# A transformer block on one core: value projection moved, fills removed, strip copies and strip transposes reordered

## The chip, the cores and the metric

The kernel runs on one core of one Trainium2 chip. The metric is the device time of one execution in microseconds (us), as the median of several runs. All times below are in us from the first instruction of the profiled execution, unless they are marked ns.

## What is computed

Eight sequences of 256 token ids go through an embedding and one transformer block of width 256 with 16 heads of 16, in float32:

```python
h = onehot(x) @ embeddings                               # (8, 256, 256)
# attention, H = 16 heads, hd = 16, rotary embedding of q and k
q, k, v = split(layernorm(h) @ w_qkv)
attn = softmax((rope(q) @ rope(k).T) * hd ** -0.5)
h = h + (attn @ v).reshape(B, N, D) @ w_proj
# mixture of experts, E = 8, the best-scored expert alone
y = layernorm(h)
chosen = argmax(y @ gate_w.T)
h = h + y + expert_w[chosen] @ y
```

## The kernel before

**Batches as a pipeline.** Each of the eight sequences is a batch `b` of NT = 2 tiles of 128 tokens. Products that need float32 accuracy are made from a high and a low part of each operand: `product` (L484) issues three matmuls for each of the two 128-row halves of the contraction. The work on a batch is spread over several steps: in step `b` TensorE makes the transposed scores of batch `b`, whose exponentials ScalarE takes (`exp`, L889), the plain scores of batch `b + 1`, whose maxima VectorE takes (`maximum`, L1027), the projections of batch `b + 2`, the end of the attention and the gate of batch `b - 1`, and the experts of batch `b - 2`. A pass numbered -1 goes before step 0, and steps 8 and 9 empty the pipeline.

**Slots set the order.** Every engine has its own program, and each walks through 16 slots per step. Tables (`FRONT`, `EARLY`, `TWO`, `FOUR` for the projections of a batch, `POST` and `LAST` for what follows the attention) name the slot in which an item is issued, on whichever engines have a part in it. Within a slot the order is that of the lines of each engine's `step`. Engines run strictly in that order and wait for one another by semaphores, so an instruction that waits holds up all that stands behind it on its engine.

**TensorE's step (L749).** Even slots hold a `visit` (L645): the scores of two heads, 8 matmuls. A visit waits for VectorE's maxima and ScalarE's exponentials of the visit before (L581, L624). In step 0 each visit is followed by fills (L491, L755), matmuls into `m_bank` whose result is not read: 3, then 4, then 1 each. Slots 5, 9 and 13, and slot 1 of the next step, hold `outputs` (L666), the product of exponentials and values for four heads; ScalarE copies its strips from `o_bank` to `o_t` (`outputs`, L897) in slots 6, 10 and 14 and in slot 1. The same bank's other half takes the transposes of the maxima (`max_transpose`, L613) in slot 3 and in slot 10 or 11; those wait for the copies of groups 1 and 3. In slot 11 of steps 0 and 1 the projection of q and k of a later batch follows, which waits for VectorE's `x_low` (L998).

**After the attention of a batch `k`,** in step `k + 1`: `o_transpose` (L681) turns the strips of tile 0 in slot 2 (`o0`) and of tile 1 in slot 4 (`o1`), both into `m_bank` except for tile 1 of batch 0 (`strips_bank`, L266), so tile 1 waits for VectorE's `o_norm` (L1042) of tile 0, which is in slot 3; `o_norm` of tile 1 is in slot 5. Then `on_transpose` (slot 6), `o_high` and `o_low` (L903, L1051), `out_project` (slot 8), `residual` and the second normalisation `g_norm` (slots 9 to 11), `y_transpose` (slot 12). A unit of experts (`experts`, L734) stands in each even slot of steps 2 to 6, in other slots from step 7 on; within a slot it comes after `o_transpose` of tile 1 and after `project_v`.

**The value projection** `project_v(b)` (L509) has 12 matmuls of 128x256. For batch 2 it stands in slot 7 of step 0 (`TWO`), goes to `f_bank` (`v_bank`, L217), and ScalarE's `values` (L850) copies it to `vals`. In step 0, slot 9, `x_transpose(3)` (L496) goes to `f_bank` too; it waits for VectorE's `xn` (L992), which in turn stands behind `max_split` (L1034) of slot 7. SyncE moves the maxima's rows and the restacked q and k by DMA (`maximum`, L292, `restack`, L314).

Of the kernel before, what the change touches and what calls it, by code (L numbers as in the profile page):

```python
# [36 lines left out]
def tower(nc, x, emb, w_qkv, w_proj, gate_w, expert_w, rope, ramp, out):  # L37
# [12 lines left out]
    with ExitStack() as ctx:  # L50
# [77 lines left out]
        def pair_of_banks(name):  # L128
# [6 lines left out]
        f_bank = bank("f_bank")  # L135
        o_bank = bank("o_bank")
        m_bank = bank("m_bank")
        e_bank = bank("e_bank")
# [37 lines left out]

        FRONT = dict(stats=-8, norm=-6, x=-5, x_low=-4, qk0=-3, qk1=-1, rotate0=-2, rotate1=0, t0=1, low0=2, t1=3, low1=4, v=5)
        EARLY = dict(stats=-12, norm=-9, x=-7, x_low=-6, qk0=-5, qk1=-4, rotate0=-3, rotate1=-2, t0=0, low0=1, t1=2, low1=3, v=5)
        TWO = dict(rotate0=0, rotate1=1, t0=2, low0=3, t1=4, low1=5, v=7)
        FOUR = dict(FRONT, stats=-10, norm=-8, x=-7, x_low=-6, qk0=-5, rotate0=-3, qk1=-2, v=-3)  # L180
        POST = dict(o0=2, o1=4, norm0=3, norm1=5, on=6, o_low=7, proj=8, residual=9, stats=10, g_norm=11,
                    y=12, y_low=13, gate=14, gate_t=15, choose=15)
        LAST = dict(o0=2, o1=2, norm0=3, norm1=3, on=4, o_low=5, proj=6, residual=7, stats=7, g_norm=8,
                    y=9, y_low=10, gate=11, gate_t=12, choose=12)
# [15 lines left out]
        def here(b, k):  # L200

            return 0 <= b + k < NB
# [12 lines left out]
            return m_bank if k in (1, 2) else f_bank  # L215

        def v_bank(k):  # L217
            return o_bank if k < 2 else e_bank if k == 4 else f_bank

        def x_parts(k):  # L220
            return (y_h[0], y_l[0]) if k == 1 else (x_h, x_l)
# [258 lines left out]
        def _(pe):  # L480
# [10 lines left out]
            def fill(o, n):  # L491

                for i in range(n):
                    mm(o[:, :], wqkv_h[:, 0, 0:P], wqkv_h[:, 0, 0:512], start=True, stop=True)
# [14 lines left out]
            def project_v(b, tiles=range(NT)):  # L509
                if tiles[0] > 0:  # L510
                    pass
                elif b == 4:
                    wait(pe, xl_ok, b + 1)
                    wait(pe, on_ok, NT)
                elif b >= 2:
                    wait(pe, qkl_ok, (b - 1) * NT + NT)
                elif b == 1:
                    wait(pe, v_ok, b)
                else:
                    pe.wait_ge(z_in, z_copied(1, 3))  # L520
                x_h, x_l = x_parts(b)
                for t in tiles:
                    m = product(v_bank(b)[:, t * D:(t + 1) * D], lambda c: x_h[:, c, t, :], lambda c: x_l[:, c, t, :],
                                lambda c: wqkv_h[:, c, 2 * D:3 * D], lambda c: wqkv_l[:, c, 2 * D:3 * D])
                if tiles[-1] == NT - 1:
                    m.then_inc(v_ps, 1)
# [86 lines left out]
            def max_transpose(b, u):  # L613

                wait(pe, o_ok, (b - 1) * GROUPS + (4 if u else 2))
                if b == 0:
                    pe.wait_ge(v_ok, 2)
                wait(pe, ml_ok, b * 2 + u + 1)
                for t in range(NT):
                    m = tr(o_bank[0:16, N + t * P:N + (t + 1) * P].bitcast(F32R),  # L620
                           max_parts[:, u, t, :, :, :].rearrange("p i a j -> p (i a j)"), ident_r[:, :])
                m.then_inc(mt_ps, 1)
# [126 lines left out]
            def step(b, p):  # L749
                for s in range(SLOTS):  # L750
                    g_at = SLOTS * b + s
                    if s % 2 == 0:
                        visit(b, s // 2)
                        if b == 0:
                            fill(m_bank, 3 if s == 0 else 4 if s == 2 else 1)  # L755
                    if here(b, 0) and s == 3:
                        max_transpose(b, 1)
                    if here(b, 1) and s == maxima_slot(b + 1):
# [74 lines left out]
            fill(m_bank, 1)  # L833
            visit(-1, 7)
            project_qk(2, 1, [1])
            fill(m_bank, 2)
            steps(step)


        @block.scalar  # L840
        def _(act):
# [80 lines left out]
            def step(b, p):  # L922
                for s in range(SLOTS):
                    g_at = SLOTS * b + s
                    if here(b, 0) and s % 2 == 0:
                        exp(b, s // 2)
                    if here(b, 0) and s == 3:
                        max_row(b, 1)
                    if here(b, -1) and s == 1:
                        outputs(b - 1, 3)  # L930
                    for k in batches(front, "x", g_at):
                        x_high(k)
                    if here(b, 0) and s in (6, 10, 14):
                        outputs(b, (s - 6) // 4)
                    for k in batches(post, "on", g_at):
                        o_high(k)
                    for t in range(NT):
                        for k in batches(front, f"t{t}", g_at):
                            qk_high(k, t)
                        for k in batches(front, f"low{t}", g_at):  # L940
                            qk_high_again(k, t)
                    for k in batches(front, "v", g_at):
                        values(k)
                    if here(b, 1) and s == maxima_slot(b + 1):
                        max_row(b + 1, 0)
                    for k in batches(post, "y", g_at):
                        y_high(k, k % 2)
                    for k in batches(post, "gate", g_at):
                        gate_row(k)
                    if b < 2 and s % 4 == 1:  # L950
                        expert_weights(4 * b + s // 4)
# [309 lines left out]
```

## Time and profile before

| | us |
|---|---|
| median of 3 runs | 303.5 |
| lowest and highest | 303.13, 305.42 |
| profiled execution, device time | 303.43 |
| its span, first to last instruction | 301.6 |

The page of the profile gives TensorE 278.1 us of busy time (92% of the span), VectorE 242.2 (80%), ScalarE 132.5 (44%) and GpSimd 88.7 (29%). The granted TensorE clock is 1.000 over the span. Of the chain that ended last 63% lies on TensorE, 25% on VectorE and 5% on ScalarE. TensorE's matmuls are pipelined and overlap, so a busy share of 92% says that something is always in flight, not that it works at its peak. A visit can be found in a timeline as a pair of rows L640 and L599; a row's idle time in brackets is that of its engine just before it, with the instruction that ended it. From visit 0 to visit 0, steps 3 and 4 take 33.0 us each, step 0 takes 22.3.

### The profile page before, as it was taken

How to read it: one execution, taken by the hardware profiler on the slowest of the kernel's cores; microseconds unless marked ns; L12 is line 12 of the kernel's file. 1: busy time of each engine (PE TensorE's matmuls, PEld its weight loads, DVE VectorE, ACT ScalarE, POOL GpSimd, SP SyncE). 2: the span in 40 equal slices, each digit the busy share in tenths (PEclk: the TensorE clock that was granted, in tenths of full speed). 3: DMA queues.
4: the chain of work that ended last, by engine and by line, in shares of the span. 5: the costliest groups of instructions: out<-in, count | busy, mean ns of one | idle time of the engine just before them, and what ended most of it. 6: DMA issues, size and time to landing. Idle time of an engine off the chain costs nothing.

```text
span 301.6 us, 5654 instructions
## 1 busy us (share of the span) xinstructions
PE 278.1 (92%) x2068; PEld 199.2 (66%) x2068; DVE 242.2 (80%) x602; ACT 132.5 (44%) x271; POOL 88.7 (29%) x105
## 2 busy tenths in 40 slices
PE   2798999898898999999999999999999999999895
PEld 2577666555576676777667776777667666667584
DVE  8698899698879898879978798869888965557765
ACT  3165438667465442553336443643433455330100
POOL 5735628184334042502240132202200300210400
PEclk9999999999999999999999999999999999999999
DMA  4440625905800840176003900193010010010011
GB/s 120 147 190 8 168 51 95 132 8 98 120 1 13 147 65 2 43 120 95 4 2 90 149 12 2 37 158 54 5 36 2 2 37 3 3 35 0 0 37 35
DMA packets 10803, 17.55 MB, mean 58 GB/s; under 512 B 2024, under 2 KB 4883, under 8 KB 10648
## 3 DMA queue, kind: packets, MB, share of 16 engines
q1 hardware_dynamic: 9988, 16.62, 27.5%
q0 software_dynamic: 768, 0.55, 0.8%
q8 instruction: 17, 0.28, 0.5%
q14 instruction: 10, 0.08, 0.1%
q10 hardware_dynamic: 20, 0.02, 0.0%
HBM read 5.30 MB, written 2.10 MB: 25 GB/s over the span
## 4 chain that ended last, share of the span: by engine, by line
PE 63%; DVE 25%; ACT 5%; issue 4%; POOL 2%; DVEq 0%; POOLq 0%
PE e_bank L488 19%; PE f_bank L488 10%; PE o_bank L676 9%; DVE neg_max L1030 6%; PE t_pair L640 5%; DVE acc L1128 4%; PE s_pair L488 4%; PE m_bank L488 3%; PE s_pair L599 2%; PE m_bank L690 2%; PE m_bank L722 2%; ACT probs L894 1%; POOL h L376 1%; PE m_bank L698 1%; ACT parts L843 1%
## 5 line engine op out<-in xcount | busy, mean ns | idle before, releaser
L894 ACT ACTIVATE probs<-t_pair 128x512 f32<-128x512 f32 x128 | 69.5, 595 | 85.9 <-PE t_pair L640 85.5
L1030 DVE TENSOR_REDUCE neg_max<-s_pair 128x2 f32<-128x512 f32 x120 | 76.9, 683 | 9.7 <-PE s_pair L599 9.5
L640 PE MATMUL t_pair<-stacks 50*128 50x256 f32 x256 | 46.8, 308 | 1.6 <-DVE neg_max L1030 0.8
L640 PEld LDWEIGHTS t_pair<-stacks 50*128 50x128 f32 x256 | 32.8, 185 | 23.4 <-issue 21.5
L599 PE MATMUL s_pair<-stacks 48*128 48x256 f32 x240 | 44.8, 309 | 0.2 <-ACT stacks L843 0.2
L488 PE MATMUL e_bank<-ew_h,y_h 128*128 128x512 f32 x92 | 40.2, 437 | 1.9 <-DVE acc L1128 1.5
L1128 DVE SCALAR_TENSOR_TENSOR acc<-e_bank,mask,acc 128x256 f32<-128x256 f32 x66 | 28.9, 479 | 11.6 <-PE e_bank L488 11.5
L488 PE MATMUL e_bank<-ew_l,y_h 128*128 128x512 f32 x92 | 36.3, 395 | 0.0
L488 PE MATMUL e_bank<-ew_h,y_l 128*128 128x512 f32 x92 | 36.2, 393 | 0.0
L406 POOL TENSOR_TENSOR qk<-rope_a,rope_b 128x512 f32<-128x512 f32 x16 | 20.8, 1300 | 48.3 <-DVE rope_b L1017 48.3
L676 PE MATMUL o_bank<-probs,vals 128*32 128x256 f32 x512 | 34.3, 385 | 0.0
L599 PEld LDWEIGHTS s_pair<-stacks 48*128 48x128 f32 x240 | 31.3, 185 | 0.9 <-issue 0.4
L488 PEld LDWEIGHTS e_bank<-ew_h,y_h 128*128 128x128 f32 x92 | 17.3, 188 | 9.0 <-DVE acc L1128 3.9
L412 POOL TENSOR_SCALAR g_ve<-g_mv 128x2 f32<-128x2 f32 x8 | 2.0, 246 | 68.9 <-DVE g_mv L986 68.9
L676 PEld LDWEIGHTS o_bank<-probs,vals 128*32 128x32 f32 x512 | 13.4, 109 | 12.4 <-issue 5.4
L488 PEld LDWEIGHTS e_bank<-ew_l,y_h 128*128 128x128 f32 x92 | 17.3, 188 | 4.0
L376 POOL DMA_INDIRECT h<-in_emb,ids x16 | 17.8, 1110 | 5.6 <-issue 3.1
L843 ACT ACTIVATE o_t<-o_bank 128x256 f32<-128x256 f32 x32 | 12.5, 390 | 14.7 <-PE o_bank L676 14.7
L488 PEld LDWEIGHTS e_bank<-ew_h,y_l 128*128 128x128 f32 x92 | 17.4, 189 | 2.1
L488 PE MATMUL f_bank<-wqkv_h,x_h 128*128 128x512 f32 (+1 forms) x42 | 15.1, 360 | 0.6 <-DVE x_l L1001 0.4
L423 POOL TENSOR_TENSOR res<-acc 128x256 f32<-128x256 f32 x14 | 10.3, 735 | 16.4 <-DVE acc L1128 16.4
L488 PE MATMUL f_bank<-wqkv_h,x_l 128*128 128x512 f32 (+1 forms) x42 | 14.3, 341 | 0.0
(182 smaller groups left out, 554.5 us busy)
## 6 DMA issues: line engine op xcount, KB each, us to landing
stacks<-parts SPq DMA_DIRECT2D x36, 256.0 KB, 6.8
ew_raw<-in_expert_w SPq DMA_DIRECT2D x1, 2048.0 KB, 8.4
out<-res SPq DMA_DIRECT2D x7, 256.0 KB
stacks<-parts SPq DMA_DIRECT2D x12, 128.0 KB, 3.3
probs<-in_w_qkv SPq DMA_DIRECT2D x2, 384.0 KB, 3.1
stacks<-max_rows SPq DMA_DIRECT2D x30, 8.0 KB
h<-in_emb,ids POOLq DMA_INDIRECT x16, 7.3
probs<-in_w_proj SPq DMA_DIRECT2D x1, 256.0 KB
```

The costliest lines, as they stand in the source:

```text
L376: g.indirect_dma_start(h0[:, j, :], None, emb, bass.IndirectOffsetOnAxis(ap=ids[:, j:j + 1], axis=0), bounds_check=V - 1, oob_is_err=False ...
L406: g.tensor_tensor(turned, rope_a[:, t, :, :].rearrange("p (g j) d -> p g j d", j=j), rope_b[:, t, :, :].rearrange("p (g j) d -> p g j d", ...
L423: g.tensor_tensor(res[:, t, :], acc[:, 0, t, :], acc[:, 1, t, :], ALU.add).then_inc(res_ok, 1)
L488: m = mm(o, a(c), w(c), start=(c == 0 and n == 0), stop=(c == C - 1 and n == 2))
L599: m = mm(scores_pair(b, v)[:, half, t * N:(t + 1) * N], stacks[b % STACKS][r:r + KS, pair, 0, t * P:(t + 1) * P], stacks[b % STACKS][r:r + ...
L640: m = mm(t_pair[:, half, c * N:(c + 1) * N], stacks[b % STACKS][r:r + KM, pair, 1, c * P:(c + 1) * P], stacks[b % STACKS][r:r + KM, pair, ...
L676: m = mm(o_bank[STRIP * j:STRIP * (j + 1), 0:N], vals_flat[b % VALS][:, at:at + STRIP], probs[:, (4 * g + j) % RING, c, :], start=(c == 0) ...
L690: m = tr(strips_bank(b, t)[:, g * P:(g + 1) * P], o_t[:, g, t * P:(t + 1) * P], ident[:, :])
L843: return nc.scalar.activation(o, i, ACT.Copy)
L894: nc.scalar.activation(probs[:, (2 * v + half) % RING, :, :].rearrange("p c n -> p (c n)"), t_pair[:, half, :], ACT.Exp, scale=SCALE).then ...
L1030: v.tensor_reduce(neg_max[:, k // 4, :, 4 * half + k % 4], scores_pair(b, k)[:, half, :].rearrange("p (t n) -> p t n", t=NT), AX.X, ALU.ma ...
L1128: v.scalar_tensor_tensor(out=acc[:, j, t, :], in0=y, scalar=mask[:, p, t, e:e + 1], in1=base[:, t, :] if u == 0 else acc[:, j, t, :], op0= ...
```

## The change

Four edits.

1. `project_v(2)` leaves slot 7 of step 0. Its tile 0 is issued just before step 0, in place of two fills, and its tile 1 after visit 0, in place of three fills. It goes to `o_bank` instead of `f_bank`, waits for the values of batch 1 to be copied, and ScalarE copies its result after the first exponentials of step 0. The max transpose of slot 3 in step 0, which writes to `o_bank`, waits for that copy.
2. Of step 0's other fills (4 after visit 1, one after each of the six visits after it) three remain after visit 1 and none elsewhere.
3. ScalarE's copies of the output strips in slots 6, 10 and 14 of all steps stand before the exponentials of their slot instead of after them.
4. The strips of tile 1 are turned in slot 5 instead of slot 4, for all batches but the last.

```diff
--- before.py
+++ after.py
@@ -176,9 +176,9 @@
 
         FRONT = dict(stats=-8, norm=-6, x=-5, x_low=-4, qk0=-3, qk1=-1, rotate0=-2, rotate1=0, t0=1, low0=2, t1=3, low1=4, v=5)
         EARLY = dict(stats=-12, norm=-9, x=-7, x_low=-6, qk0=-5, qk1=-4, rotate0=-3, rotate1=-2, t0=0, low0=1, t1=2, low1=3, v=5)
-        TWO = dict(rotate0=0, rotate1=1, t0=2, low0=3, t1=4, low1=5, v=7)
+        TWO = dict(rotate0=0, rotate1=1, t0=2, low0=3, t1=4, low1=5)
         FOUR = dict(FRONT, stats=-10, norm=-8, x=-7, x_low=-6, qk0=-5, rotate0=-3, qk1=-2, v=-3)
-        POST = dict(o0=2, o1=4, norm0=3, norm1=5, on=6, o_low=7, proj=8, residual=9, stats=10, g_norm=11,
+        POST = dict(o0=2, o1=5, norm0=3, norm1=5, on=6, o_low=7, proj=8, residual=9, stats=10, g_norm=11,
                     y=12, y_low=13, gate=14, gate_t=15, choose=15)
         LAST = dict(o0=2, o1=2, norm0=3, norm1=3, on=4, o_low=5, proj=6, residual=7, stats=7, g_norm=8,
                     y=9, y_low=10, gate=11, gate_t=12, choose=12)
@@ -215,7 +215,7 @@
             return m_bank if k in (1, 2) else f_bank
 
         def v_bank(k):
-            return o_bank if k < 2 else e_bank if k == 4 else f_bank
+            return o_bank if k < 3 else e_bank if k == 4 else f_bank
 
         def x_parts(k):
             return (y_h[0], y_l[0]) if k == 1 else (x_h, x_l)
@@ -512,9 +512,9 @@
                 elif b == 4:
                     wait(pe, xl_ok, b + 1)
                     wait(pe, on_ok, NT)
-                elif b >= 2:
+                elif b >= 3:
                     wait(pe, qkl_ok, (b - 1) * NT + NT)
-                elif b == 1:
+                elif b >= 1:
                     wait(pe, v_ok, b)
                 else:
                     pe.wait_ge(z_in, z_copied(1, 3))
@@ -614,7 +614,7 @@
 
                 wait(pe, o_ok, (b - 1) * GROUPS + (4 if u else 2))
                 if b == 0:
-                    pe.wait_ge(v_ok, 2)
+                    pe.wait_ge(v_ok, 3)
                 wait(pe, ml_ok, b * 2 + u + 1)
                 for t in range(NT):
                     m = tr(o_bank[0:16, N + t * P:N + (t + 1) * P].bitcast(F32R),
@@ -751,8 +751,10 @@
                     g_at = SLOTS * b + s
                     if s % 2 == 0:
                         visit(b, s // 2)
-                        if b == 0:
-                            fill(m_bank, 3 if s == 0 else 4 if s == 2 else 1)
+                        if b == 0 and s == 0:
+                            project_v(2, [1])
+                        if b == 0 and s == 2:
+                            fill(m_bank, 3)
                     if here(b, 0) and s == 3:
                         max_transpose(b, 1)
                     if here(b, 1) and s == maxima_slot(b + 1):
@@ -833,7 +835,7 @@
             fill(m_bank, 1)
             visit(-1, 7)
             project_qk(2, 1, [1])
-            fill(m_bank, 2)
+            project_v(2, [0])
             steps(step)
 
 
@@ -922,16 +924,18 @@
             def step(b, p):
                 for s in range(SLOTS):
                     g_at = SLOTS * b + s
+                    if here(b, 0) and s in (6, 10, 14):
+                        outputs(b, (s - 6) // 4)
                     if here(b, 0) and s % 2 == 0:
                         exp(b, s // 2)
+                    if b == 0 and s == 0:
+                        values(2)
                     if here(b, 0) and s == 3:
                         max_row(b, 1)
                     if here(b, -1) and s == 1:
                         outputs(b - 1, 3)
                     for k in batches(front, "x", g_at):
                         x_high(k)
-                    if here(b, 0) and s in (6, 10, 14):
-                        outputs(b, (s - 6) // 4)
                     for k in batches(post, "on", g_at):
                         o_high(k)
                     for t in range(NT):
```

## Rows read from the trace of the kernel before

**Rows 1.** Step 0: busy time by engine, granted clock, DMA share, GB/s

```profile
40.40:63.10 22.70, 20.22 (x168) 13.46 (x167) 19.35 (x38) 15.02 (x31) 11.27 (x11) 1.00 0.49 76
```

**Rows 2.** Timeline of TensorE in step 0: start, length, instruction, idle before

```profile
41.64 0.96 PE L494 MATMUL m_bank<-wqkv_h 128*128 128x512 f32 x3
...
42.77 0.35 PE L640 MATMUL t_pair<-stacks 50*128 50x256 f32 x1 [0.17 <-DVE neg_max L1030]
...
43.80 1.20 PE L494 MATMUL m_bank<-wqkv_h 128*128 128x512 f32 x4
...
49.76 0.28 PE L488 MATMUL f_bank<-wqkv_h,x_h 128*128 128x256 f32 x1
...
51.29 0.38 PE L640 MATMUL t_pair<-stacks 50*128 50x256 f32 x1
...
52.89 0.63 PE L506 MATMUL f_bank<-ident,xn 128*128 128x128 f32 x4 [0.43 <-DVE xn L995]
...
54.45 0.38 PE L640 MATMUL t_pair<-stacks 50*128 50x256 f32 x1
...
55.12 0.50 PE L494 MATMUL m_bank<-wqkv_h 128*128 128x512 f32 x1
...
56.40 0.29 PE L620 MATMUL o_bank<-ident_r,max_parts 128*16 128x128 f32 x2 [0.78 <-ACT o_t L843]
...
63.06 0.35 PE L640 MATMUL t_pair<-stacks 50*128 50x256 f32 x1 [0.33 <-DVE neg_max L1030]
```

**Rows 3.** Timeline of VectorE in step 0

```profile
46.10 0.69 DVE L1022 TENSOR_TENSOR parts<-f_bank,parts 128x512 fp32r<-128x512 f32 x1 [0.49 <-ACT parts L843]
...
50.67 1.21 DVE L1037 CAST max_parts<-neg_max 128x16 fp32r<-128x16 f32 x1
...
58.64 1.29 DVE L1030 TENSOR_REDUCE neg_max<-s_pair 128x2 f32<-128x512 f32 x2 [2.33 <-PE s_pair L599]
```

**Rows 4.** Timeline of ScalarE in step 0

```profile
49.36 1.06 ACT L894 ACTIVATE probs<-t_pair 128x512 f32<-128x512 f32 x2
...
51.40 0.60 ACT L843 ACTIVATE vals<-f_bank 128x512 f32<-128x512 f32 x1 [0.70 <-PE f_bank L488]
...
55.95 0.39 ACT L843 ACTIVATE o_t<-o_bank 128x256 f32<-128x256 f32 x1
```

**Rows 5.** Timeline of TensorE, step 1, slots 10 to 12

```profile
80.67 0.29 PE L620 MATMUL o_bank<-ident_r,max_parts 128*16 128x128 f32 x2 [1.21 <-ACT o_t L843]
...
83.01 0.66 PE L714 MATMUL m_bank<-ident,yn 128*128 128x128 f32 x4
```

**Rows 6.** Timeline of VectorE, the same stretch

```profile
79.06 0.66 DVE L1001 TENSOR_TENSOR x_l<-f_bank,x_h 128x512 fp32r<-128x512 f32 x1
...
81.29 0.74 DVE L1070 TENSOR_SCALAR yn<-h,g_mv,g_rs 128x256 f32<-128x256 f32 x2 [0.38 <-POOL g_rs L414]
```

**Rows 7.** L690's idle time by releaser (us, times); TensorE in step 3

```profile
  DVE o_n L1047: 4.9, 10
...
129.16 0.66 PE L690 MATMUL m_bank<-ident,o_t 128*128 128x128 f32 x4 [0.40 <-DVE o_n L1047]
...
132.56 1.07 PE L676 MATMUL o_bank<-probs,vals 128*32 128x256 f32 x16
```

**Rows 8.** Timeline of VectorE in step 3, slot 5

```profile
131.24 0.88 DVE L1128 SCALAR_TENSOR_TENSOR acc<-e_bank,mask,acc 128x256 f32<-128x256 f32 x2 [0.34 <-PE e_bank L488]
```

**Rows 9.** Timeline of ScalarE in step 3, slot 6

```profile
134.10 1.09 ACT L894 ACTIVATE probs<-t_pair 128x512 f32<-128x512 f32 x2 [0.83 <-PE t_pair L640]
```

**Rows 10.** Timeline of TensorE in step 7, slot 8

```profile
255.63 0.38 PE L488 MATMUL m_bank<-wp_h,o_h 128*128 128x256 f32 x1 [0.25 <-DVE o_l L1053]
```

**Rows 11.** Fills of the start: ns min/median/max, first and last start

```profile
L494 PE MATMUL s_pair<-wqkv_h x13: 387/592/767, 5.3 to 9.6; 128*128 128x512 f32 x13
```

**Rows 12.** Busy times and granted clock, 10.0 to 13.4

```profile
10.00:13.40 3.40, 1.80 (x9) 1.28 (x10) 2.44 (x8) 0.70 (x2) 2.88 (x4) 1.00 0.60 165
```

**Rows 13.** Timeline of SyncE's queue at the end of step 0

```profile
57.12 1.37 SPq L297 DMA_DIRECT2D stacks<-max_rows  x2
```

## The prediction

> **What bounds the kernel now.** I read the profile in this order: the busy shares by stretch, the chain that ended last, then the timelines of TensorE, VectorE and ScalarE beside each other for one step of each kind (step 0, step 1, one of the alike steps 2 to 6, step 7), each time asking who ended TensorE's idle time. In a stretch of 22.7 us that holds step 0, TensorE is busy 20.22 us and VectorE 19.35 us [rows 1], so neither alone sets the pace; the chain changes from one to the other. Part of TensorE's busy time there is fills, matmuls whose result nobody reads: 3 after visit 0, 4 after visit 1, one after each later visit, 13 in step 0 and 2 more just before it [rows 2]. From step 2 on TensorE has next to no idle time but 0.4 us per step before the transposes of the second tile's strips [rows 7]. So TensorE sets the end from step 2 on, and in steps 0 and 1 a chain through all three engines does.
>
> **Step 0, slots 0 to 4.** The projection v(2) (12 matmuls of 128x256) leaves slot 7, where it holds TensorE from 49.76 to the next visit at 51.29, 1.53 us, together with its bank change from f_bank to o_bank. Its first half takes the place of two fills before visit 0, its second half that of the three fills after it. Three fills last 0.96 us there, and half of v is 0.77 us, so TensorE is at visit 1 no later; and visit 1 ended an idle time of 0.17 us that VectorE's maxima released [rows 2], so this costs nothing; without that cover it would cost at most the 0.3 us by which 0.77 exceeds two fills (0.48). ScalarE gets the copy into vals, 0.60 us [rows 4], between the first exponentials: the second pair comes some 0.3 us later. Visit 2 waits for that pair, but only 2 us after it; nothing is lost. The maxima's transpose of slot 3 now waits for that copy too; behind it TensorE's whole queue would stand, but the copy ends near 43.2 and the transpose is due at 45. The fourth fill after visit 1 goes: 1.20 minus 0.96 is 0.24 us. That one counts, since ScalarE's high part, and behind it VectorE (idle 0.49 us at 46.10 [rows 3]), waits for the transposes issued after the fills. I take 0.2 us.
>
> **Step 0, slots 6 to 10.** Without v and the fill, visit 4 no longer waits for TensorE but for the exponentials of visit 3 (49.36 plus 1.06 us [rows 4]): its second half can go near 50.5, where before the whole visit began at 51.29. That gain of nearly 1 us is not kept: VectorE's split of the maxima (50.67, 1.21 us for a 128x16 cast [rows 3]) and its xn stand in front of the x transposes of slot 9 at 52.89, which TensorE waited for by 0.43 us anyway [rows 2]. What is kept there is the 0.2 us from above (bounds: nothing, if the long cast ends when it ended before; the whole 1.2 us, if it shrinks to the ordinary length).
>
> Now the copies. In slot 10 the max transpose waits for the copy of output group 1. Before, that copy stood behind both exponentials of visit 5: it began at 55.95, and TensorE, done with the visit at 55.12 and with one fill after it, sat idle 0.78 us until 56.40 [rows 2, 4]. The strips are finished when visit 5 begins (54.45), so a copy in front takes 54.5 to 54.9, less the 0.2, and ends before the visit does. The transpose follows the visit: 56.40 minus 55.12 is 1.28 us, minus 0.03 of latency, plus the 0.2: 1.45 us. VectorE had been idle 2.33 us behind this (58.64 [rows 3]), so it takes over the whole 1.45. From there to visit 0 of step 1 (63.06) VectorE is busy without a break; the fills of slots 12 and 14 are worth nothing. **Step 0: 1.45 us.**
>
> **Step 1.** In slot 6 the copy in front lets o_high start 0.26 us earlier (a copy's 0.39 us less the overlap), of which the split of the maxima leaves about 0.2. In slot 10 TensorE waited 1.21 us for the copy of group 1, until 80.67 [rows 5]. Without that, the next limits are VectorE's x_low, done at 79.72, which releases qk(4,0), and yn, done at 82.03, which releases the y transposes (83.01 before) [rows 5, 6]. The latter leaves 0.9 us. **Step 1: 0.9 + 0.2 = 1.1 us.**
>
> **Steps 2 to 6, the second tile's strips.** The two tiles' strips share m_bank, so the second turn must wait until VectorE has normalised the first, and in slot 4 TensorE stood for that: 0.40 us at 129.16; the view lists ten such waits, five on the matmul row and five on the weight row [rows 7], one pair for each of the five steps. With the turn in slot 5 the unit of experts of slot 4 comes first; it waits for nothing here, since the select before it is over. Then come the four transposes, v(k) and the output group. Nothing is added; 0.40 us of standing goes. Who waits for the strips now? VectorE's second normalisation, which stands behind a select begun at 131.24 [rows 8] that itself now starts 0.35 us sooner; experts (1.5 us) and transposes (0.6) end some 2.1 us after the visit, near 130.9, and that select ends near 131.7. VectorE then waits for visit 3 in any case, so TensorE keeps its gain. In step 1 no work lies between slots 4 and 5 and the order stays; in step 7 likewise, for its experts stand in odd slots. **5 x 0.40 = 2.0 us** (bounds: 0, if the wait only changes its name; 2.5, if each step saves the wait and 0.1 us of restart after it).
>
> **The copies in steps 2 to 7.** A copy ahead of the exponentials could delay them. It does not: the output group begins at 132.56 and lasts 1.07 us, the exponentials begin at 134.10 after 0.83 us of idle time [rows 7, 9]; the copy needs 0.26 us before the next can follow and starts near 133.7. It has no gain either, but in step 7: there the out projection stood 0.25 us for o_low [rows 10], which hangs on ScalarE's o_high behind that copy. **0.25 us.**
>
> **Sum:** 1.45 + 1.1 + 2.0 + 0.25 = 4.8 us. The profiled execution took 303.43 us (span 301.6); minus 4.8 is 298.6. The median of the three runs is 303.5, so the same number holds for it.
>
> **The rivals.** *The strips' gain moves on* (0.12): VectorE's second normalisation is late and the next transposes wait as long. Then 303.4 - 2.8 = 300.6. For it: VectorE is also nearly full; against it: it waits for visit 3 after that normalisation.
> *Step 0 gives little* (0.10): the transfer of the maxima's rows, issued from 57.12 in 1.37 us behind the restack's transfers [rows 13], is needed (by visit 0 of step 1, 63.06) 1.45 us earlier but issued only 1 us earlier, since the row copy still stands behind both exponentials; or the cast takes back what came. Step 0 and 1 then give 1.2 instead of 2.5: 299.9.
> *The clock falls once* (0.08). TensorE's work from 49.3 to 52.7 shrinks to one visit of 0.7 us, and an idle time of about 1.7 us stands before the x transposes. The thinnest stretch of the trace, 1.80 us busy of 3.40, was granted 1.00 (2.4 GHz) [rows 12], so the rows speak against it but do not reach that far. The price: of the 13 fills of the start the last began 4.3 us after the first, with a median of 592 ns against 387 at the fastest [rows 11]; 12 spacings of 0.24 us would be 2.9. So 1.4 us and a little for the shorter work between: 1.6 us, and 300.2.
> The Trainium skill (TensorE: Matmul & The Clock Gate, Part 1) says that half rate is the default and that recent activity releases it, which speaks against taking fills out; by that rule this case comes about, and with it those 300.2 us.
> *Slower than before* (0.04): the clock falls there and stays low. From 52.7 to about 60 TensorE sets the pace with some 7 us of work. At 1.2 GHz it costs its own length again: 7 us, so 305.6. It decides from 4.8 us of work at the low level on.
> *More than summed* (0.08): the long cast disappears or the fills had cost others: 1.2 us more, 297.4.
>
> **How the numbers follow.** The forecast has the remaining 0.58, with its own range of 298.0 to 299.2. With the rivals, 297.3 to 300.7 leaves out the lasting clock fall and tails, under 2 in 10. A measurement of this kernel tells about 1% from no change, 3 us here: faster means below 300.5. The forecast, the larger gain, the little step 0 and half of the cases at 300.2 and 300.6 lie there, and some unknown is taken off: 0.81. Within 1%: 0.14. Slower: 0.05.
>
> **What the profile after would show.** Visit 0 of step 1 near 61.6. No wait for o_t before the max transposes of slot 10. No o_n idle before m_bank's strips in steps 2 to 6, and periods of 32.6 us in place of 33.0 (129.16 to its like). Granted clock 1.00 from 49 to 56. The prediction falls if that clock is lower, if visit 0 of step 1 waits for the transfer, or if a new wait of 0.3 us or more stands in slots 5 or 6 of steps 2 to 6.

## The result, and the profile after

| us | before | after |
|---|---|---|
| median of 10 runs each, on one chip | 303.56 | 300.38 |
| lowest and highest of after | | 299.73, 302.31 |
| profiled execution of after | 303.43 | 300.52 |
| its span | 301.6 | 298.7 |
| granted clock over its span | 1.000 | 0.989 |

The ratio is 0.9884, with a 95% interval from 0.9861 to 0.9907: the change saves 3.2 us of the 4.8 that were summed. The time lies inside the range (297.3 to 300.7), but not where the likeliest case put it (298.0 to 299.2). It lies where the rival "the clock falls once" did, at 300.2, and that rival had a chance of 0.08.

The page of the profile of after has a row of the granted clock (the span in 40 slices of 7.5 us, tenths of full speed), and it shows one dip. Before, it has none.

```profile
PEclk9999998699999999999999999999999999999999
```

The windows around it, of the kernel after (window, length, busy us of TensorE, its weight loads, VectorE, ScalarE and GpSimd with instruction counts, granted clock, DMA share, GB/s), to be set beside [rows 1], which reads 1.00 for all of step 0:

```profile
44.40:48.40 4.00, 3.69 (x40) 2.30 (x38) 3.74 (x9) 3.48 (x8) 3.53 (x4) 1.00 0.07 18
48.40:50.40 2.00, 1.09 (x12) 0.65 (x8) 1.97 (x5) 1.96 (x5) 1.92 (x3) 0.99 0.65 171
50.40:52.40 2.00, 0.85 (x6) 0.53 (x4) 1.97 (x5) 1.20 (x2) 1.32 (x2) 0.50 1.08 153
52.40:54.40 2.00, 1.85 (x12) 1.11 (x16) 1.30 (x4) 0.73 (x2) 0.00 (x0) 0.50 1.06 152
54.40:56.40 2.00, 2.00 (x20) 1.12 (x12) 0.69 (x2) 0.91 (x3) 1.27 (x1) 0.50 1.04 154
56.40:58.40 2.00, 2.00 (x12) 1.37 (x8) 1.19 (x2) 1.19 (x3) 0.00 (x0) 0.80 1.05 153
58.40:60.40 2.00, 2.00 (x14) 1.56 (x14) 1.31 (x3) 1.28 (x3) 0.00 (x0) 1.00 0.28 37
```

The clock is at its lower level, 1.2 GHz (0.50), from about 50.4 to 57, and back at 2.4 GHz behind that. TensorE's timeline of the same stretch shows what stood before the fall and what it cost. These rows of after answer to [rows 2]:

```profile
49.97 0.35 PE L640 MATMUL t_pair<-stacks 50*128 50x256 f32 x1 [0.82 <-ACT probs L896]
50.17 0.28 PE L640 MATMUL t_pair<-stacks 50*128 50x256 f32 x1
50.46 0.55 PE L640 MATMUL t_pair<-stacks 50*128 50x256 f32 x1
50.81 0.42 PE L640 MATMUL t_pair<-stacks 50*128 50x256 f32 x1
...
52.55 1.08 PE L506 MATMUL f_bank<-ident,xn 128*128 128x128 f32 x4 [1.30 <-DVE xn L999]
53.57 1.94 PE L676 MATMUL o_bank<-probs,vals 128*32 128x256 f32 x16
...
56.59 0.38 PE L620 MATMUL o_bank<-ident_r,max_parts 128*16 128x128 f32 x2
...
63.52 0.35 PE L640 MATMUL t_pair<-stacks 50*128 50x256 f32 x1 [0.98 <-DVE neg_max L1034]
```

Two idle times, 0.82 and 1.30 us, frame visit 4 (49.97). The clock fell between the two halves of this visit: the first two matmuls have their ordinary 0.35 and 0.28 us, the next two take 0.55 and 0.42. So in this execution the second gap came too late to be a cause of the fall. The x transposes behind it take 1.08 us where they took 0.63, the output group 1.94 where it takes 1.07 at the full clock. The wait for `o_t` in front of L620 (0.78 before) is gone, as forecast, yet L620 starts at 56.59 instead of 56.40: what the copies gave back, the clock took. Visit 0 of step 1 starts at 63.52, before it was 63.06.

From there on the sum comes out. I took the starts of the 32 output groups (L676, four to a batch) in both traces and their differences, after minus before. For the groups of step 0 they go from -0.38 to +0.44 and for those of step 1 from +0.45 to -0.69. At the first group of steps 2 to 6, which stands just behind the strips, they are -1.12, -1.46, -1.90, -2.27 and -2.61, and in step 7 they go from -2.63 to -2.89. So step 1 gives 1.13 us (1.1 summed), the five steps with strips 1.92 (2.0 summed), step 7 0.26 (0.25 summed). TensorE and VectorE after, in step 1, slot 10, which answer to [rows 5] and [rows 6]:

```profile
79.62 0.29 PE L620 MATMUL o_bank<-ident_r,max_parts 128*16 128x128 f32 x2
80.01 0.51 PE L488 MATMUL f_bank<-wqkv_h,x_h 128*128 128x512 f32 x1
...
82.33 0.66 PE L714 MATMUL m_bank<-ident,yn 128*128 128x128 f32 x4
```

```profile
79.29 0.66 DVE L1005 TENSOR_TENSOR x_l<-f_bank,x_h 128x512 fp32r<-128x512 f32 x1
...
81.54 0.74 DVE L1074 TENSOR_SCALAR yn<-h,g_mv,g_rs 128x256 f32<-128x256 f32 x2 [0.39 <-POOL g_rs L414]
```

The 1.21 us for `o_t` are gone. `x_l` ends at 79.95 and releases the next projection at 80.01, `yn` ends at 82.28 and releases the y transposes at 82.33, 0.68 us earlier than before, although the step was entered 0.45 us late. These are the two limits that the prediction named.

The strips of the second tile, in the groups of instructions of L690 (busy, mean ns, idle before), stood 1.9 us for `o_n` on the matmul row before. After:

```profile
L690 PE MATMUL m_bank<-ident,o_t 128*128 128x128 f32 x56 | 8.5, 274 | 0.0
```

Two successive steps of TensorE after, at that place. Between their starts lie 32.55 us, where 33.0 lay before [rows 7] and 32.6 was forecast:

```profile
129.13 0.60 PE L690 MATMUL m_bank<-ident,o_t 128*128 128x128 f32 x4
...
161.68 0.60 PE L690 MATMUL m_bank<-ident,o_t 128*128 128x128 f32 x4
```

VectorE behind them has the slack that the prediction leaned on. Its second normalisation is done at 131.2, and it waits 1.44 us for visit 3. It answers to [rows 8]:

```profile
130.81 0.42 DVE L1051 TENSOR_TENSOR o_n<-m_bank,o_rs 128x256 f32<-128x256 f32 x1
132.67 1.29 DVE L1034 TENSOR_REDUCE neg_max<-s_pair 128x2 f32<-128x512 f32 x2 [1.44 <-PE s_pair L599]
```

### The profile page after: what moved, and what is told of

Read it like the earlier page. It is cut to its first block, busy times and chain, and to the rows that moved or that the text cites. A ratio compares the mean times of both kernels' runs of the same rounds, so it can differ in the third digit from the quotient of the medians.

```text
span 298.7 us, 5630 instructions
## 1 busy us (share of the span) xinstructions
PE 277.7 (93%) x2056; PEld 199.2 (67%) x2056; DVE 241.7 (81%) x602; ACT 134.4 (45%) x271; POOL 88.4 (30%) x105
## 4 chain that ended last, share of the span: by engine, by line
PE 69%; DVE 24%; ACT 3%; issue 2%; POOL 1%; DVEq 0%; POOLq 0%
PE e_bank L488 21%; PE f_bank L488 10%; PE o_bank L676 9%; PE t_pair L640 7%; DVE neg_max L1034 5%; PE s_pair L488 4%; DVE acc L1132 4%; PE s_pair L599 3%; PE m_bank L488 2%; PE m_bank L690 2%; PE f_bank L561 2%; PE m_bank L722 2%; PE m_bank L698 1%; DVE xn L999 1%; DVE h L1198 1%
## 5 line engine op out<-in xcount | busy, mean ns | idle before, releaser
L640 PE MATMUL t_pair<-stacks 50*128 50x256 f32 x256 | 47.9, 312 | 2.9 <-DVE neg_max L1034 1.0
L640 PEld LDWEIGHTS t_pair<-stacks 50*128 50x128 f32 x256 | 33.5, 188 | 24.9 <-issue 22.5
L599 PE MATMUL s_pair<-stacks 48*128 48x256 f32 x240 | 46.0, 313 | 0.2 <-ACT stacks L845 0.2
L676 PE MATMUL o_bank<-probs,vals 128*32 128x256 f32 x512 | 35.1, 393 | 0.0
L599 PEld LDWEIGHTS s_pair<-stacks 48*128 48x128 f32 x240 | 32.0, 188 | 0.9 <-issue 0.4
L676 PEld LDWEIGHTS o_bank<-probs,vals 128*32 128x32 f32 x512 | 13.6, 110 | 12.5 <-issue 5.6
L488 PE MATMUL f_bank<-wqkv_h,x_h 128*128 128x512 f32 (+1 forms) x38 | 14.5, 382 | 0.7 <-DVE x_l L1005 0.6
L494 PE MATMUL s_pair<-wqkv_h 128*128 128x512 f32 x26 | 8.7, 485 | 5.6 <-ACT wqkv_h L845 5.6
```

The source lines that it names most:

```text
L488: m = mm(o, a(c), w(c), start=(c == 0 and n == 0), stop=(c == C - 1 and n == 2))
L599: m = mm(scores_pair(b, v)[:, half, t * N:(t + 1) * N], stacks[b % STACKS][r:r + KS, pair, 0, t * P:(t + 1) * P], stacks[b % STACKS][r:r + ...
L640: m = mm(t_pair[:, half, c * N:(c + 1) * N], stacks[b % STACKS][r:r + KM, pair, 1, c * P:(c + 1) * P], stacks[b % STACKS][r:r + KM, pair, ...
L676: m = mm(o_bank[STRIP * j:STRIP * (j + 1), 0:N], vals_flat[b % VALS][:, at:at + STRIP], probs[:, (4 * g + j) % RING, c, :], start=(c == 0) ...
```

## The experiments

The theory was: the missing 1.9 us are the clock, which fell because TensorE had too little work around visit 4; all other terms are right. The rival: the transfers (DMA share 1.05 in those windows) or VectorE hold step 0 back and the clock is only a witness. Each kernel is changed from the one after, unless said otherwise. Ratios are to the kernel before on the same chip, with 95% intervals.

**Fills put back in the two gaps.**

```diff
-                        if b == 0 and s == 2:
-                            fill(m_bank, 3)
+                        if b == 0 and s in (2, 6, 8):
+                            fill(m_bank, {2: 3, 6: 3, 8: 6}[s])
```

> The changed kernel with 3 fills added after visit 3 and 6 after visit 4 of step 0, where TensorE stood idle 0.82 and 1.30 us. Theory A (the idle stretch let the clock fall, and matmuls at 1.2 GHz cost about 2 us): granted clock 1.00 from 50 to 58 us, the outputs of slot 9 last 1.07 us again instead of 1.94, visit 0 of step 1 at 61.6 instead of 63.5, and 298.4 us in all. Theory B (those matmuls were slow for another reason, the restack's transfers running at the same time): they stay slow, and the fills change nothing or cost up to 0.3 us: 300.4 to 300.7 us.

Measured: 298.56 (298.33 to 298.69), ratio 0.9836 [0.9802, 0.9869], clock 1.0 in each of four runs. That is the 298.6 of the prediction. Its windows and its timeline of TensorE:

```profile
50.40:52.40 2.00, 1.98 (x11) 1.27 (x11) 2.00 (x4) 1.08 (x2) 1.15 (x1) 1.00 1.07 144
52.40:54.40 2.00, 2.00 (x26) 1.25 (x28) 1.73 (x3) 1.35 (x3) 0.16 (x1) 1.00 1.05 150
```

```profile
50.71 1.65 PE L494 MATMUL m_bank<-wqkv_h 128*128 128x512 f32 x6
52.38 0.63 PE L506 MATMUL f_bank<-ident,xn 128*128 128x128 f32 x4
52.94 1.07 PE L676 MATMUL o_bank<-probs,vals 128*32 128x256 f32 x16
54.61 0.29 PE L620 MATMUL o_bank<-ident_r,max_parts 128*16 128x128 f32 x2
...
61.28 0.35 PE L640 MATMUL t_pair<-stacks 50*128 50x256 f32 x1 [0.98 <-ACT probs L896]
```

The DMA share is the same 1.07 and 1.05, and nothing waits on it: the rival falls. Nine matmuls whose result nobody reads make the kernel 1.8 us faster by the medians (1.5 by the two ratios, each against the kernel before on its own chip). Visit 0 of step 1 is at 61.28, 1.78 earlier than before; 0.57 of that already stands at the first output group of step 0, ahead of any of the copies: 0.24 for the fill that went, and the rest within what such starts differ by from run to run (0.6 us, below). The Trainium skill (TensorE: Matmul & The Clock Gate, Part 1) says that the half rate is the default and recent activity releases the full one; this pair of traces agrees, 0.50 against 1.00.

**Step 0 left as it was before** (value projection in slot 7, all fills back), the copies and the strips changed.

```diff
-        TWO = dict(rotate0=0, rotate1=1, t0=2, low0=3, t1=4, low1=5)
+        TWO = dict(rotate0=0, rotate1=1, t0=2, low0=3, t1=4, low1=5, v=7)
...
-                        if b == 0 and s == 0:
-                            project_v(2, [1])
-                        if b == 0 and s == 2:
-                            fill(m_bank, 3)
+                        if b == 0:
+                            fill(m_bank, 3 if s == 0 else 4 if s == 2 else 1)
```

> Step 0 as in the kernel before (projection in slot 7, all 15 fills), with the copies first and the second tile turned in slot 5. Theory A: the clock stays at 1.00; 2.0 us from steps 2 to 6, 0.26 from step 7, 1.1 from step 1, and 1.2 from slot 10 of step 0 come off: 303.5 - 4.6 = 298.9 us, so undoing this part makes the changed kernel faster by 1.5 us. Theory B (the step 0 edit as such was worth something and the slow matmuls come from the transfers): slow matmuls here too, 300.4 us or more.

Measured: 299.20 (299.17 to 299.33, four runs), ratio 0.9855 [0.9822, 0.9888], 0.3 above what was expected. So the edits of step 0, taken alone, made the kernel slower: 300.38 with them, 299.20 without. With the gaps filled they give 0.6 us.

**The strips of tile 1 back in slot 4.**

```diff
-        POST = dict(o0=2, o1=5, norm0=3, norm1=5, ...
+        POST = dict(o0=2, o1=4, norm0=3, norm1=5, ...
```

> The changed kernel with the second tile's strips turned in slot 4 again. If steps 2 to 6 each gained the 0.40 us wait for the first tile's normalisation, that wait is back five times: 300.4 + 2.0 = 302.4 us, and the output groups of steps 2 to 6 fall behind those of the changed kernel by 0.4 us a step. If the gain of these steps came from the copies, nothing changes: 300.4 us.

Measured: 302.5 (301.98 to 304.48, ten runs), ratio 0.9974 [0.9948, 1.0]; the edit is worth 2.1 us. The group of L690 in this kernel shows where:

```profile
L690 PE MATMUL m_bank<-ident,o_t 128*128 128x128 f32 x56 | 8.8, 279 | 1.9 <-DVE o_n L1051 1.9
```

Its output groups run 0.74 us ahead of the kernel before when step 2 begins and 0.61 ahead when step 6 ends, where those of the kernel after go from 0.69 to 2.61 ahead. So the edit's whole worth lies in these steps.

**The copies back behind the exponentials.**

```diff
-                    if here(b, 0) and s in (6, 10, 14):
-                        outputs(b, (s - 6) // 4)
                     if here(b, 0) and s % 2 == 0:
                         exp(b, s // 2)
...
                         x_high(k)
+                    if here(b, 0) and s in (6, 10, 14):
+                        outputs(b, (s - 6) // 4)
```

> The changed kernel with the strip copies behind the exponentials again. Expected: steps 2 to 6 unchanged; step 7 gives back 0.26 us, step 1 1.1 us (TensorE stands for the copy in slot 10), and step 0 about 0.7 us, since the max transpose of slot 10 waits for both exponentials (1.1 us) less what the visit at half clock covers: 300.4 + 2.1 = 302.5 us. The rival: the copies matter only in step 1, 301.5 us.

Measured: 304.37 (303.46 to 305.74, ten runs), ratio 1.0014 [0.9986, 1.0043]. I had expected 302.5. The copies are worth 4.0 us here, not the 2.1 that I gave them. Its windows and TensorE's timeline:

```profile
56.40:58.40 2.00, 0.98 (x8) 0.63 (x4) 1.19 (x2) 1.53 (x4) 0.00 (x0) 0.50 1.04 140
58.40:60.40 2.00, 2.00 (x6) 1.32 (x4) 0.00 (x0) 0.08 (x1) 0.00 (x0) 0.50 0.43 66
60.40:62.40 2.00, 2.00 (x11) 1.47 (x11) 0.87 (x2) 0.85 (x2) 0.00 (x0) 0.58 0.01 4
```

```profile
57.68 0.38 PE L620 MATMUL o_bank<-ident_r,max_parts 128*16 128x128 f32 x2 [1.02 <-ACT o_t L845]
57.86 0.74 PE L488 MATMUL f_bank<-wqkv_h,x_h 128*128 128x512 f32 x1
58.40 0.63 PE L488 MATMUL f_bank<-wqkv_h,x_l 128*128 128x512 f32 x1
```

The wait for `o_t` is back and stands inside the low stretch. The clock fell later here, at about 51.9, in the middle of 1.59 us of idle time behind visit 4, and the low level lasts until about 62 instead of 57: some 10 us instead of 7. A 128x512 matmul takes 0.63 us, where it takes 0.39 to 0.40 at the full clock. So in this execution the wait cost its own length and went with a longer slow stretch. The mean clocks of all ten runs fit: they are 0.977 to 0.989, against 0.983 to 0.994 in the kernel after. To see the copies' own worth, I did the same with the gaps filled:

> The kernel with filled gaps (3 fills after visit 3, 6 after visit 4), but the strip copies behind the exponentials again: the copies' own worth, with the clock held. By my sum they give 1.25 us in step 0, 1.1 in step 1 and 0.25 in step 7, so 298.5 + 2.6 = 301.1 us at a clock of 1.00. If the 4 us that copies_after_exp lost against the changed kernel were the copies' own, it would be 302.5 us.

Measured: 301.64 (301.41 to 302.67, five runs), ratio 0.9946 [0.9915, 0.9977]. The mean clock is 0.998 in the profiled, fastest run (1.00 through step 0 and 1) and 0.994 in the others, so I compare the profiled executions, 301.41 and 298.33: the difference is 3.1 us with the clock held (the medians give 3.1 too). In the two traces, counted from the first output group of step 0, the copies give 1.28 us in step 0, 1.12 in step 1 and 0.27 in step 7. That is 2.67, against 2.6 in the sum (1.25 of the 1.45, 1.1 and 0.25). The other 0.4 us stand ahead of that group, where no copy differs: in eight profiled kernels whose program is the same up to there it starts anywhere from 46.49 to 47.12. The waits that the copies remove, in this kernel's TensorE, step 0 and step 1:

```profile
56.33 0.29 PE L620 MATMUL o_bank<-ident_r,max_parts 128*16 128x128 f32 x2 [1.21 <-ACT o_t L845]
...
80.59 0.29 PE L620 MATMUL o_bank<-ident_r,max_parts 128*16 128x128 f32 x2 [1.21 <-ACT o_t L845]
```

**Which removal brought the clock down?** Five kernels. First the single fills back after visits 2 to 7 (`fill(m_bank, 3 if s == 2 else 1)` in every even slot from 2 on), with the projection still moved:

> The changed kernel with one fill (0.22 us) after each of visits 2 to 7 of step 0, as the kernel before had them; the projection stays before and after visit 0. The stretch from visit 3 to the x transposes then holds about 1.2 us of matmuls in 3.3. If it is the projection's move that let the clock fall, the clock falls here too: 300.4 us and outputs of slot 9 that last 1.94 us. If the single fills were what held it, the clock stays: 298.4 us. I lean to the first, 6 to 4.

Measured: 299.52, ratio 0.9876 [0.982, 0.9931], and the four runs fall apart: 298.63 and 298.73 at a mean clock of 0.998 to 0.999, 300.31 at 0.994, 301.84 at 0.988. Then the six fills after visit 4 alone, the gap before it left open:

> The changed kernel with 6 fills after visit 4 alone; the idle time of 0.8 us between visits 3 and 4 stays. The kernel before has idle times of 0.8 to 1.2 us at a clock of 1.00, so I expect 1.00 here: 298.6 us. If the fall needs both gaps filled, 300.4 us.

Measured: 299.94, ratio 0.9876 [0.9839, 0.9913]: 298.94 at clock 1.0, 299.8 and 300.08 at 0.993, 301.04 at 0.989. I expected 298.6 and missed in three runs of four. The other way round, three fills after visit 3, none after visit 4, and three after visit 7, so that no idle time stands before visit 0 of step 1 (`if b == 0 and s in (2, 6, 14): fill(m_bank, 3)`):

> Three fills after visit 3 fill the first gap (0.82 us) as in the kernel with both gaps filled, three after visit 7 close the idle time before visit 0 of step 1, and the second gap, between visit 4 and the x transposes, stays open at about 1.3 us. In the profiled execution of the kernel after the clock fell inside visit 4, ahead of that second gap. Theory A, the first gap and the thin work before it are enough and are the cause: the clock stays up, 298.6 to 298.8 us at a mean clock of 1.0 in all runs. Theory B, either gap is enough: falls at about 52 us in some or all of the runs, those runs at a mean clock of 0.98 to 0.994 and 299.8 to 300.4 us. The share of runs at the lower clock tells how near this stretch is to the edge.

Measured: 299.29, ratio 0.9876 [0.9838, 0.9913], six runs: 298.35, 298.56 and 298.62 at clock 1.0, twice 299.95 at 0.994, and 302.23 at 0.989. This is what theory B forecast, that either gap is enough in some of the runs, but it is not shown: where the clock fell in the runs without a profile can't be seen, and the kernel before, which has neither gap, was at 0.994 in five of 19 runs. What is shown are the two ends. With both gaps open the mean clock was 0.977 to 0.994 in thirty of thirty runs (ten each of the kernel after and of the two with the strips or the copies put back). With both filled and nothing else changed it stayed up in four of four, and in four more with three fills after visit 7 (below). Filled gaps are no guarantee either: with the late copies four of five runs were at 0.994, and the kernel with one fill less after visit 1 (below) had one such run in five, the profiled one, whose clock fell behind visit 0 of step 1, at about 63. The profiled execution is one of those at 1.0. Its TensorE is idle for longer than in the kernel after, and nothing happens:

```profile
52.47 0.63 PE L506 MATMUL f_bank<-ident,xn 128*128 128x128 f32 x4 [1.59 <-DVE xn L999]
```

Then the projection back in slot 7, but without the single fills:

> Step 0 with the projection in slot 7 and its fills before step 0 and after visits 0 and 1 as before, but none after the later visits; copies first, second tile in slot 5. It takes the fills out and leaves the projection in the gap. If the projection's move was the cause of the low clock, the clock stays at 1.00 and the fill after visit 5, which stood ahead of the max transpose, is saved: 299.2 - 0.2 = 299.0 us. If the missing fills were the cause, the clock falls: 300.5 to 301 us.

Measured: 298.88 (298.56 to 299.5), ratio 0.9826 [0.9793, 0.9858]. Three of the four runs are at clock 1.0, in spite of 1.00 us idle before the x transposes, against none of ten in the kernel after. So neither the moved projection alone (single fills kept, two runs of four low) nor the missing single fills alone (one of four) takes the clock down in every run; the two together did. Which of them weighs more, so few runs do not show. The profiled run, the slowest of the four, shows a fall at another place, after the idle time before visit 0 of step 1, where the fills after visits 6 and 7 used to be. TensorE's timeline and the windows of this kernel:

```profile
52.73 0.63 PE L506 MATMUL f_bank<-ident,xn 128*128 128x128 f32 x4 [1.00 <-DVE xn L995]
...
61.62 0.35 PE L640 MATMUL t_pair<-stacks 50*128 50x256 f32 x1 [0.98 <-DVE neg_max L1030]
```

```profile
60.40:62.40 2.00, 0.92 (x10) 0.57 (x10) 1.93 (x5) 1.32 (x4) 2.00 (x3) 1.00 0.00 0
62.40:64.40 2.00, 2.00 (x20) 1.14 (x22) 2.00 (x3) 1.52 (x3) 1.84 (x2) 0.73 0.02 4
64.40:66.40 2.00, 2.00 (x17) 1.09 (x10) 1.38 (x3) 1.19 (x3) 1.41 (x2) 0.50 0.10 22
```

Last, both gaps around visit 4 filled and three fills more after visit 7:

> Filled gaps and 3 more fills after visit 7, where the profiles show 1 us of idle time before visit 0 of step 1. In two_fills_then_gaps and v_slot7_no_single_fills the clock fell there in the profiled run. VectorE releases visit 0, so the fills should cost nothing: 298.5 us, clock 1.00 in every run. If they delay visit 0: up to 0.3 us more.

Measured: median 298.76 (lowest 298.33), ratio 0.9846 [0.983, 0.9863], against 298.56 without those three. In its profiled execution (302.97) the clock fell at about 26 and 38 us, ahead of any edit, so it shows nothing on step 1; the other four lie between 298.33 and 298.77. From run to run, then, the three fills bring nothing that can be told where the clock stayed up already.

**VectorE's long instruction.** In the trace before, the cast of the maxima takes 1.21 us [rows 3] where others of its kind take 0.18. After, the cast takes 0.18 and the instruction behind it 1.21. VectorE and GpSimd of the kernel after:

```profile
50.33 0.18 DVE L1041 CAST max_parts<-neg_max 128x16 fp32r<-128x16 f32 x1
50.55 1.21 DVE L1043 TENSOR_TENSOR max_parts<-neg_max,max_parts 128x16 fp32r<-128x16 f32 x1
```

```profile
50.46 1.26 POOL L429 TENSOR_TENSOR ew_l<-ew_raw,ew_h 128x512 fp32r<-128x512 f32 x1
```

In both traces the instruction that VectorE starts just behind GpSimd's 128x512 subtraction (`ew_l`) ends with it. The next kernel has one fill less after visit 1, so that the split is over 0.2 us sooner against it:

> As fills_in_gaps (3 fills after visit 3, 6 after visit 4), but with 2 fills after visit 1 instead of 3. VectorE's idle time of 0.26 us at 45.8 should go, and its split of the maxima then ends before GpSimd's ew_l begins near 50.4, so that the 1.21 us instruction there takes 0.17. If so, xn and what hangs on it come up to 1.2 us sooner and the kernel takes 297.3 us. The rival: the second part of the split still falls behind ew_l's start and stands for it, 298.4 us.

Measured: 298.20 (298.1 to 299.86, five runs), ratio 0.9808 [0.9776, 0.984]. I had expected 298.4, or 297.3 if the long instruction disappeared. The split took 0.17 us, and then `xn` took it over. VectorE of this kernel, whose GpSimd began `ew_l` at 50.94:

```profile
50.79 0.17 DVE L1043 TENSOR_TENSOR max_parts<-neg_max,max_parts 128x16 fp32r<-128x16 f32 x1
50.99 1.71 DVE L999 TENSOR_SCALAR xn<-h,f_mv,f_rs 128x256 f32<-128x256 f32 x2
```

So the wait has to be taken from GpSimd's side. In the next kernel its second `ew_l` of step 0 waits for `xn`; against the kernel just shown TensorE has four fills less after visit 4, where the gap is now shorter, and three more after visit 7:

```diff
+                    if b == 0 and s == 5:
+                        wait(pool, f_normed, 4 * NT)
...
-                        if b == 0 and s == 2:
-                            fill(m_bank, 3)
+                        if b == 0 and s in (2, 6, 8, 14):
+                            fill(m_bank, {2: 2, 6: 3, 8: 2, 14: 3}[s])
```

> Filled gaps with 2 fills after visit 1, 3 after visit 3, 2 after visit 4, 3 after visit 7, and GpSimd's second ew_l made to wait until VectorE's xn of slot 7 is done. In two_fills_then_gaps that ew_l stood beside xn, which took 1.71 us instead of 0.73. If the two exclude one another, xn takes 0.73 us again, the x transposes come about 1 us sooner and the kernel takes 297.4 us. Rival 1: VectorE or the transfer of the maxima's rows takes it back before visit 0 of step 1, 298.2 us. Rival 2: xn was long for its own sake, 298.2 us with xn at 1.7 us.

Measured: 297.33 (297.28 to 297.39, four runs at clock 1.0), ratio 0.9803 [0.9786, 0.9819]. It is the fastest of all kernels here. VectorE and GpSimd:

```profile
50.30 0.74 DVE L1001 TENSOR_SCALAR xn<-h,f_mv,f_rs 128x256 f32<-128x256 f32 x2
```

```profile
51.12 1.28 POOL L429 TENSOR_TENSOR ew_l<-ew_raw,ew_h 128x512 fp32r<-128x512 f32 x1 [0.85 <-DVE xn L1001]
```

`xn` takes 0.74 us, the x transposes start at 51.19 instead of 52.38, and visit 0 of step 1 at 60.59 instead of 61.28. The fills differ too: they end at 51.17, just behind `xn` (51.04), as with filled gaps they ended at 52.36, just behind `xn` (52.23). So GpSimd's wait freed `xn`, and the gain reached TensorE because the fills behind visit 4 were cut with it.

## Why the prediction was right, and where not

**The step that failed is the term of step 0.** It was summed at 1.45 us gained; measured, visit 0 of step 1 came 0.46 us later, so the term was 1.9 us too high. The mechanism behind it was right: with the clock at 1.00 (the kernel with filled gaps) the copies give 1.28 us in step 0, and the total is the 298.6 of the forecast. What failed is its condition, "granted clock 1.00 from 49 to 56". That the time lies inside the stated range is luck in part: it is there because the range was widened for the rivals, not by the sum. The prediction saw that the removals leave one visit between two idle times, and gave the fall of the clock 0.08, on the ground of a stretch with 1.80 us busy of 3.40 at a clock of 1.00 [rows 12]. That stretch lay at another place, behind other work, and said nothing of this one. In ten runs of ten the mean clock of after is 0.983 to 0.994, so the 0.08 was far too low.

**The price of the fall** was put at 1.6 us from the fills of the start. Measured: 300.38 - 298.56 = 1.82 (1.5 by the ratios). The size was right, though the rows did not show that the clock made those first fills slow: from 5.3 to 9.6 the column of the granted clock reads 1.00. The idle time of 1.7 us that was foreseen before the x transposes is 1.30, with 0.82 more before visit 4.

**Step 0's own edits.** "The fills of slots 12 and 14 are worth nothing" holds for the time they cover, not for the clock: without them visit 0 of step 1 stands behind 0.98 us of idle time instead of 0.33, and in two kernels the profiled execution lost the clock there. The fourth fill after visit 1 was right in size: from visit 1 to the x transposes the kernel after takes 9.88 us and before 10.12, the 0.2 us that were kept in the sum. The cast's 1.21 us did not go with it; they passed to the subtraction. Of the two bounds given for the cast, the upper one (1.2) was reached only where GpSimd was made to wait: 1.16 us by the output group of slot 9, and 297.33 in all, about the 297.4 of the rival "more than summed".

**Step 1, steps 2 to 6, step 7**: 1.1, 2.0 and 0.25 summed, 1.13, 1.92 and 0.26 measured, each also by an experiment that undid one edit. The signs named for the profile were there: no `o_t` wait, no `o_n` idle, a period of 32.55 us, no new wait in slots 5 and 6. Only the clock, and with it the 61.6 for visit 0 of step 1 (63.52), were not.

**The other rivals.** The row transfer is issued at 57.62 and nothing waits for it: it plays no part. The strips' gain did not move on. The clock did not stay low.

## What to carry to other kernels

Count what a removed filler matmul covers twice: once for the time, once for the clock. When work leaves a slot, list TensorE's idle times on both sides of what remains, and when two of them now stand around one short piece of work, take the slower clock as a likely case, and fill both gaps in the same edit. A filler in front of something that TensorE waits for anyway is free; here nine of them brought 1.8 us. And when a short instruction of VectorE takes several times its usual length, look for what GpSimd started just before it, and order GpSimd's instruction behind the chain; to shift VectorE by 0.2 us only hands the wait to its neighbour.

## What the runs showed of the hardware that I had not expected

**The longest idle time does not decide on the clock.** One of 1.59 us left it at 1.00 in the profiled execution of the kernel with the gap after visit 4 open, and 1.21 us before L620 at 56.33 did in the one with filled gaps and late copies. In the kernel after it fell behind 0.82 us, within the next visit (about 50.4), likewise with the strips back in slot 4 (about 50.1); with the copies back it passed 0.69 us there and fell within the 1.59 us that followed (about 51.9). It also goes from run to run: with single fills the same program was at full clock in two runs of four, with one gap open in one of four and three of six. The kernel before is not safe either: of 19 runs beside the first experiments, most took 303.1 to 303.8 us, and five took 305.0 to 305.4, all five with a mean clock of 0.994.

**A low stretch was longer with a wait inside it**: from 50.4 to 57 without the wait for `o_t`, from 51.9 to near 62 with it, though the wait is 1.02 us long. These are one trace each; that the wait is the cause is argued, not shown. The same edit was worth 4.0 us here and 3.1 where the gaps were filled.

**Several of VectorE's instructions were held to the end of one of GpSimd's.** A 128x16 cast took 1.21 us, a 128x16 subtraction 1.21, and `xn` 1.71 for two pieces that need 0.72 to 0.74, each beside the same 128x512 `ew_l` of 1.26 to 1.28 us. It is not `ew_l` alone: behind visit 0 of step 1, in the kernel after, the same subtraction takes 1.21 us at 64.24, beside GpSimd's 128x512 `qk` (64.12, 1.31 us), and no kernel here removed that wait. The Trainium skill (SBUF — State Buffer, SBUF: two separate sides) says that VectorE and GpSimd share a pair of ports as an exclusive lock for a whole instruction, and that the other then fully blocks; VectorE takes it for instructions in a two-port mode or with two inputs in SBUF. The traces agree as far as they reach: the subtraction has both inputs in SBUF, while VectorE's maxima out of PSUM kept their usual 1.29 us beside `ew_l` (started at 55.02 before and at 54.51 with filled gaps), and so did its 128x512 `parts` with one input in PSUM (0.68 us at 48.42 in the kernel after). In which mode the cast and `xn` ran, no trace shows. GpSimd's 128x2 `f_rs` (0.72 us) did not lengthen the cast beside it, 0.18 us. Which forms block which was not tried further.
